# A decoder in one launch: ScalarE takes over the normalising of the state-space layer, and the passage to the next mixer is put in a new order

## The chip, the cores and the metric

One core of a Trainium2 chip runs the whole program. Its engines are named as in the profile: PE (TensorE, with its weight loads as PEld), DVE (VectorE), ACT (ScalarE), POOL (GpSimd) and SP (SyncE, which issues the DMAs). The metric is the device time of one execution in microseconds (us); lower is better.

## The reference

Six layers stand one behind the other, each as `x = layernorm(x + layer(x))`, on `x` of 16 batches, 128 tokens, 256 features. The fourth, the state-space layer, is the one that changes:

```python
zxbcdt = u @ W_in                                 # z, xBC, dt
xBC = silu(conv)                                  # causal conv of 4 taps
y, _ = ssd(x * dt[..., None], A * dt, Bh, Ch, 32)
y = y + x * D[None, None, :, None]
y = y.reshape(b, s, D_SSM) * silu(z)
var = jnp.mean(jnp.square(y), axis=-1, keepdims=True)
y = y * jax.lax.rsqrt(var + EPS) * norm_scale
return y @ W_out

def _layernorm(x, axis=-1, eps=1e-05):
    m = jnp.mean(x, axis=axis, keepdims=True)
    v = jnp.var(x, axis=axis, keepdims=True)
    return (x - m) / jnp.sqrt(v + eps)
```

The fifth layer, mixer two, multiplies keys and values per head, convolves them (a Toeplitz matrix product), multiplies by the query and sums. The sixth is a quantised feed-forward layer with a Hadamard transform.

## The kernel before

Everything is on chip: `X` holds the tokens of all 16 batches with tokens in the partitions, `XT` the same turned round. Each layer is a set of small functions, one per operation and engine, and each engine calls them in an order written out in the code. Engines work strictly in that order and meet only through semaphores: a function first waits for counts, then issues one instruction (or a few) that raises its own count. So an instruction that waits also holds up all that stands behind it on its engine.

The state-space layer works on groups of two batches. `step(i)` of an engine does the projection of group i (ten units on PE: six with the convolution's taps, four for the gate) and, beside it, the later parts of the groups before. Below, a is the first and b the second batch of the group whose scan step i prepares. The steps 2 to 7 run in a loop; `begin` and `end` write out what lies ahead of them and behind.

What happens to a batch in the parts that matter here, with lines of the profiled kernel:

- GpSimd makes the exponents (`args`, L1503) in a tile that lies in MIX. ScalarE clips them (`floor`, L1277) and takes the exponential (`decay`, L1283). VectorE multiplies by C times B (`matrix`, L1390). PE then scans (L1156).
- PE turns x back (L1135), ScalarE keeps it (`keep_xs`, L1271), GpSimd multiplies by dt (`x_dt`, L1537) and by D (`skip`, L1529).
- VectorE adds the skip (L1399) and multiplies by the gate (`gated`, L1408). ScalarE squares (L1290), GpSimd adds the squares in two instructions (`add_squares`, L1518 and L1520), PE sums (L1165), VectorE makes the variance (L1415) and GpSimd takes the root (`root`, L1511).
- PE multiplies by W_out (`out_product`, L1175), VectorE scales and adds X into tile Y (`residual`, L1423), then takes the statistics (L1429, L1435). GpSimd adds eps and takes the power -1/2 (`rstd`, L541 and L543). VectorE subtracts the mean and multiplies (`norm_x`, L549) from Y into X, with two Y tiles by turns. PE turns X (`x_turn`, L1185) and ScalarE keeps it in XT (L1296).
- In each unit ScalarE takes the product out of its bank with the fourth tap (`tap3`, L1249), and VectorE adds the three others (`taps`, L1376). The gate's units end in a Silu on ScalarE (L1258). Exp and Silu need different tables, so ScalarE loads a table twice per step.

In `end`, the last batches of the state-space layer are mixed with the first 18 of the 32 items of mixer two. An item is two products of keys and values on GpSimd (L632), six matmuls on PE (L655 to L657), two multiplications by the query (L673) and a sum (L684) on VectorE. Item 0 needs the first eight batches of XT, item 16 all of them. The keys' tile has three buffers. Behind item 17 the last layer begins, its first instruction on PE being L1616. That layer already normalises in the way that the change brings in (L1741 on ScalarE, L2040 on GpSimd).

The change touches tile Y and the new tile NR, `norm_x`, `residual`, `stats`, `aggregate`, `rstd`, and the three written orders of `step` and `end`.

Of the kernel before, what the change touches and what calls it, by code (L numbers as in the profile page):

```python
# [1054 lines left out]
def state_space(ch, T, d, s, before):  # L1055
# [38 lines left out]
    def tensor(pe):  # L1094
# [237 lines left out]

    def vector(dve):
# [83 lines left out]
        def residual(n):  # L1417
# [880 lines left out]
```

## Time and profile before

| | us |
|---|---|
| runs, median of 3 (lowest, highest) | 795.59 (793.16, 796.11) |
| profiled execution, device time | 795.49 |
| its span, first to last instruction | 793.5 |
| PE busy | 719.3 (91%) |
| DVE busy | 638.7 (80%) |
| POOL busy | 545.4 (69%) |
| ACT busy | 400.2 (50%) |
| state-space steps 2 to 7 | about 412 to 521 |
| passage to mixer two, to the first L1616 | 521 to 589.13 |

Busy shares are means over the whole program. In the two stretches named last several engines are nearly full at once, so what bounds them is read from the order of single instructions, not from the shares. Matmuls are pipelined and their ends are modelled, so PE's busy time is somewhat above its real need. A row of a timeline gives the start, the length, the instruction and, in brackets, the idle time ahead of it where that is long enough to be listed.

### The profile page before, as it was taken

To read this page: it belongs to the slowest core of one execution; us is meant where nothing else is said; L and a number is where in the kernel's file an instruction comes from. 1 tells how busy PE (TensorE), PEld (TensorE's weight loads), DVE (VectorE), ACT (ScalarE), POOL (GpSimd) and SP (SyncE) were. 2 spreads that over 40 slices of the span, in tenths; PEclk is the share of its full clock that TensorE was granted. 3 is DMA by queue.
4 is the path that set the end of the run, shared out by engine and by line. 5 is a ranking of instruction groups with operands and counts; after the bars stand their busy time and mean duration, and the time that the engine had idled before them with its cause. 6 is when DMAs were issued, how large, how long until landed. Compare 5 with 4: busy or idle time off the path is not lost. (4 is left out here: it accounts for less than half of the span.)

```text
span 793.5 us, 13405 instructions
## 1 busy us (share of the span) xinstructions
PE 719.3 (91%) x4263; PEld 496.9 (63%) x4286; DVE 638.7 (80%) x1291; ACT 400.2 (50%) x640; POOL 545.4 (69%) x785
## 2 busy tenths in 40 slices
PE   6999999999996999999859999989899898888894
PEld 5777777654442677776547777754444366666673
DVE  3878877789798777765859999969998989998754
ACT  0656566610614444444668778850100255777675
POOL 2768888977773443332147777799888788988882
PEclk9999999999998999999979999999999999999999
DMA  7900000000402300000121111103000000000001
GB/s 278 369 8 2 2 2 2 1 1 0 159 0 85 118 1 2 1 1 1 69 94 54 54 55 54 54 5 119 1 0 1 1 1 1 14 15 14 14 14 40
DMA packets 12868, 33.89 MB, mean 43 GB/s; under 512 B 2688, under 2 KB 8064, under 8 KB 11520
## 3 DMA queue, kind: packets, MB, share of 16 engines
q1 hardware_dynamic: 12800, 33.04, 11.5%
q8 instruction: 36, 0.59, 0.3%
q14 instruction: 32, 0.26, 0.1%
HBM read 30.88 MB, written 2.16 MB: 42 GB/s over the span
## 5 line engine op out<-in xcount | busy, mean ns | idle before, releaser
L1126 PE MATMUL bank<-XT,win_late 128*128 128x256 f32 x320 | 86.6, 397 | 5.7 <-DVE ss_xc L1376 5.4
L684 DVE TENSOR_REDUCE MIX<-m_pr 128x128 f32<-128x1024 f32 x64 | 77.4, 1211 | 0.7
L632 POOL TENSOR_TENSOR m_kv<-CTXT 128x512 f32<-128x512 f32 x64 | 65.0, 1039 | 10.4 <-PE bank L657 10.3
L632 POOL TENSOR_TENSOR m_kv<-XT,CTXT 128x512 f32<-128x512 f32 x64 | 67.7, 1082 | 4.2 <-PE bank L657 4.2
L1376 DVE SCALAR_TENSOR_TENSOR ss_xc<-bank,cw_late,ss_xc 128x254 f32<-128x254 f32 x144 | 66.5, 477 | 4.0 <-ACT ss_xc L1249 0.5
L1126 PEld LDWEIGHTS bank<-XT,win_late 128*128 128x128 f32 x320 | 56.1, 193 | 20.1 <-DVE ss_xc L1376 13.2
L655 PE MATMUL bank<-m_kv,toep 128*128 128x512 f32 x128 | 66.4, 600 | 1.9 <-POOL m_kv L632 1.3
L541 POOL TENSOR_TENSOR f_ve<-f_mv,eps 128x1 f32<-128x1 f32 x48 | 9.5, 198 | 81.7 <-DVE f_mv L946 61.1
L656 PE MATMUL bank<-m_kv,toep 128*128 128x512 f32 x128 | 65.4, 592 | 0.0
L657 PE MATMUL bank<-m_kv,toep 128*128 128x512 f32 x128 | 65.4, 592 | 0.0
L1686 PE MATMUL bank<-had_last,f_ht 128*128 128x256 f32 x256 | 60.7, 383 | 0.3 <-ACT f_ht L1763 0.2
L805 PE MATMUL bank<-wd,f_pmt 128*128 128x256 f32 x256 | 60.2, 382 | 0.0
L501 POOL TENSOR_TENSOR at_p<-at_p,at_mx 128x512 f32<-128x512 f32 x44 | 45.2, 1046 | 15.7 <-DVE at_mx L394 15.6
L1686 PEld LDWEIGHTS bank<-had_last,f_ht 128*128 128x128 f32 x256 | 47.4, 190 | 9.6 <-ACT f_ht L1763 2.2
L805 PEld LDWEIGHTS bank<-wd,f_pmt 128*128 128x128 f32 x256 | 46.7, 190 | 5.8
L1503 POOL TENSOR_TENSOR MIX<-CUM,MIX 128x1024 f32<-128x1024 f32 x16 | 30.3, 1900 | 26.1 <-DMA MIX<-cum_rows 18.9
L673 DVE TENSOR_TENSOR m_pr<-bank,XT 128x512 f32<-128x512 f32 x64 | 41.1, 685 | 8.4 <-PE bank L657 8.2
L673 DVE TENSOR_TENSOR m_pr<-bank,CTXT 128x512 f32<-128x512 f32 x64 | 40.8, 682 | 4.9 <-PE bank L657 4.4
L165 PE MATMUL bank<-XT,at_wqk 128*128 128x128 f32 x256 | 37.8, 299 | 6.7 <-DMA at_hmask<-hmask_dram 5.7
L657 PEld LDWEIGHTS bank<-m_kv,toep 128*128 128x128 f32 x128 | 24.3, 190 | 30.6 <-issue 30.6
L656 PEld LDWEIGHTS bank<-m_kv,toep 128*128 128x128 f32 x128 | 24.3, 190 | 30.6 <-issue 30.6
L317 ACT COPY at_pt<-bank 128x512 f32<-128x512 f32 x64 | 36.6, 590 | 11.3 <-PE bank L212 9.6
(237 smaller groups left out, 1899.6 us busy)
## 6 DMA issues: line engine op xcount, KB each, us to landing
MIX<-cum_rows SPq DMA_DIRECT2D x16, 512.0 KB, 3.7
toep<-toep_dram SPq DMA_DIRECT2D x2, 2048.0 KB, 11.8
X<-x_dram SPq DMA_DIRECT2D x1, 2048.0 KB, 12.7
CTXT<-ctxT_dram SPq DMA_DIRECT2D x1, 2048.0 KB, 17.6
out_dram<-f_o SPq DMA_DIRECT2D x16, 128.0 KB, 1.7
XT<-xT_dram SPq DMA_DIRECT2D x1, 1280.0 KB, 8.4
win_late<-win_dram SPq DMA_DIRECT2D x1, 1280.0 KB, 5.3
wgu<-wgu_dram SPq DMA_DIRECT2D x1, 1024.0 KB, 5.0
```

What stands on the lines that cost most here:

```text
L165: m = nc.tensor.matmul(b0[:, bass.ts(g, S)], wqk[:, c, bass.ts(g, P)], XT[:, c, tok(n)], start=(c == 0), stop=(c == C - 1))
L501: nc.gpsimd.tensor_tensor(v, v, MX[n % 2][:, 4 * t:4 * t + 4].unsqueeze(2).broadcast_to([P, 4, S]), ALU.subtract).then_inc(s["shifted"], 1)
L632: m = nc.gpsimd.tensor_tensor(KV[n % 3][:, c, :, :].rearrange("p (b j) i -> p b j i", b=HB), ki, vj, ALU.mult)
L655: nc.tensor.matmul(y[0][:, :], toep[:, a, 0:P], kv[0], start=True, stop=True)
L656: nc.tensor.matmul(y[1][:, :], toep[:, a, P:2 * P], kv[0], start=True, stop=False)
L657: nc.tensor.matmul(y[1][:, :], toep[:, a, 0:P], kv[1], start=False, stop=True).then_inc(s["conved"], 1)
L673: nc.vector.tensor_tensor(PR[n % 2][:, c, :, :].rearrange("p (b j) i -> p b j i", b=HB), bY[pair(n)][c][:, :].rearrange("p (b j i) -> p b ...
L684: nc.vector.tensor_reduce(head(MIX)[:, :, a, bass.ts(h, HB), :], PR[n % 2][:, :, :, :].rearrange("p c (b j) i -> p c b j i", b=HB), op=ALU ...
L805: m = nc.tensor.matmul(b6[:, 0:D], PMT[n % 2][:, r, :], wd[:, r, :], start=(r == 0), stop=(r == FC - 1))
L1126: m = nc.tensor.matmul(bX[(NU * g + n) % 3][:, 0:GS_], win[:, h, off:off + P], XT[:, h, bass.ts(g, GS_)], start=(h == 0), stop=(h == C - 1))
L1376: m = nc.vector.scalar_tensor_tensor(acc[:, :, sh:S], bank[:, :, 0:S - sh], cw[:, r, n:n + 1], acc[:, :, sh:S], ALU.mult, ALU.add)
L1686: m = nc.tensor.matmul(bV[k][:, bass.ts(r, 2 * P)], HT[:, 4 * k + 2 * r + i, :], had[:, i, :], start=(i == 0), stop=(i == 1))
```

## The change

1. `norm_x` leaves VectorE. GpSimd's `rstd` gets a third instruction, which makes -mean times the inverse deviation in a new tile NR (semaphore `offset`). ScalarE computes Y times scale plus offset into X with an Identity activation.
2. Y has three tiles instead of two, so `residual(n)` waits for the normalising of batch n-3 instead of n-2. The statistics wait until NR of two batches before is made.
3. In a step of ScalarE, `norm_x` of one batch stands between `tap3(i, 5)` and the second `keep_xs`, that of the other at the end of the step.
4. `end` has a new order on all four engines.

```diff
-    Y, ST, MV, VE, RS = two("y", [P, D]), two("st", [P, 6]), two("mv", [P, 2]), two("ve", [P, 1]), two("rs", [P, 1])
+    Y = [ch.sb(f"ss_y{k}", [P, D]) for k in range(3)]
+    NR, ST, MV, VE, RS = two("nr", [P, 1]), two("st", [P, 6]), two("mv", [P, 2]), two("ve", [P, 1]), two("rs", [P, 1])
 # scalar
+        def norm_x(n):
+            act.wait_ge(s["offset"], n + 1)
+            nc.scalar.activation(X[:, n, :], Y[n % 3][:, :], ACT.Identity, scale=RS[n % 2][:, :], bias=NR[n % 2][:, :]).then_inc(s["normed"], 1)
 # scalar, step
             tap3(i, 5)
+            norm_x(GB * (i - 3))
             keep_xs(GB * (i - 1) + 1)
...
             gate(i, 3)
+            norm_x(GB * (i - 3) + 1)
 # vector
-            upto(dve, s["normed"], n - 1)
-            nc.vector.scalar_tensor_tensor(Y[n % 2][:, :], bO[:, 0:D], RY[n % 2][:, :], X[:, n, :], ALU.mult, ALU.add).then_inc(s["out_free"], 1)
+            upto(dve, s["normed"], n - 2)
+            nc.vector.scalar_tensor_tensor(Y[n % 3][:, :], bO[:, 0:D], RY[n % 2][:, :], X[:, n, :], ALU.mult, ALU.add).then_inc(s["out_free"], 1)
 # vector, aggregate
+            upto(dve, s["offset"], n - 1)
 # vector, step
-            norm_x(GB * (i - 3))
-            norm_x(GB * (i - 3) + 1)
 # gpsimd, rstd
-            inv_std(pool, nc, T, MV[n % 2], VE[n % 2], RS[n % 2], T["eps5"], s["stats2"], s["eps_added"], s["rstd"], n)
+            upto(pool, s["normed"], n - 1)
+            k = n % 2
+            inv_std(pool, nc, T, MV[k], VE[k], RS[k], T["eps5"], s["stats2"], s["eps_added"], s["rstd"], n)
+            pool.wait_ge(s["rstd"], n + 1)
+            nc.gpsimd.tensor_scalar(NR[k][:, :], MV[k][:, 0:1], RS[k][:, :], -1.0, ALU.mult, ALU.mult).then_inc(s["offset"], 1)
 # tensor, end (first line of each)
-            scan(13); x_turn(6, 12); x_back(14); x_turn(7, 12); c_times_b(14); out_product(11); x_back(15); c_times_b(15); x_turn(8, 12); scan(14)
+            scan(13); x_turn(6, 12); x_back(14); c_times_b(14); x_turn(7, 12); out_product(11); x_turn(8, 12); c_times_b(15); x_back(15)
```

ScalarE, in the middle of a step. Names: L1249 (L1250 after) is `tap3`, L1277 (L1278) `floor`, L1271 (L1272) `keep_xs`, L1283 (L1284) `decay`. Before:

```order
L1271 COPY ss_xs<-bank 128x512
L1249 ACTIVATE ss_xc<-bank,cb_late,cw_late 128x256
L1277 ACTIVATE MIX<-MIX 128x1024
L1249 ACTIVATE ss_xc<-bank,cb_late,cw_late 128x256
L1271 COPY ss_xs<-bank 128x512
L1283 ACTIVATE MIX<-MIX 128x1024
```

After, where L1297 is the new normalising:

```order
L1250 ACTIVATE ss_xc<-bank,cb_late,cw_late 128x256
L1278 ACTIVATE MIX<-MIX 128x1024
L1250 ACTIVATE ss_xc<-bank,cb_late,cw_late 128x256
L1297 ACTIVATE X<-ss_y,ss_nr,ss_rs 128x256
L1272 COPY ss_xs<-bank 128x512
L1284 ACTIVATE MIX<-MIX 128x1024
```

The activation L1297 now stands ahead of the second `keep_xs` and so ahead of the `decay`, the table load and the square behind it.

PE, the beginning of the passage. L1156 (L1157 after) is `scan`, L1175 (L1176) `out_product`, L1185 (L1186) `x_turn`, L1135 (L1136) `x_back`, L1146 (L1147) `c_times_b`, L1165 (L1166) the sum of squares, L655 to L657 an item of mixer two. Before:

```order
L1135 MATMUL bank<-ident,ss_xc 128x128 x4
L1146 MATMUL bank<-ss_xc 128x128
L1185 MATMUL bank<-ident,X 128x128 x2
L1156 MATMUL bank<-MIX,wd 64x128 x8
L1175 MATMUL bank<-wout_late,ss_y 128x256 x4
L1156 MATMUL bank<-MIX,wd 64x128 x8
L1185 MATMUL bank<-ident,X 128x128 x2
L655 MATMUL bank<-m_kv,toep 128x512
L656 MATMUL bank<-m_kv,toep 128x512
L657 MATMUL bank<-m_kv,toep 128x512
```

After:

```order
L1136 MATMUL bank<-ident,ss_xc 128x128 x4
L1176 MATMUL bank<-wout_late,ss_y 128x256 x4
L655 MATMUL bank<-m_kv,toep 128x512
L656 MATMUL bank<-m_kv,toep 128x512
L657 MATMUL bank<-m_kv,toep 128x512
L1186 MATMUL bank<-ident,X 128x128 x2
L1157 MATMUL bank<-MIX,wd 64x128 x8
L1166 MATMUL bank<-ss_ones,ss_sq 128x1
L655 MATMUL bank<-m_kv,toep 128x512
L656 MATMUL bank<-m_kv,toep 128x512
L657 MATMUL bank<-m_kv,toep 128x512
L1157 MATMUL bank<-MIX,wd 64x128 x8
```

The item 0 of mixer two has moved ahead of both last scans, and item 1 stands between them.

GpSimd, the same place. L1503 (L1506 after) is `args`, L632 an item's product, L1537 (L1540) `x_dt`, L1529 (L1532) `skip`, L1511 (L1514) `root`, L1518 and L1520 (L1521 and L1523) `add_squares`. Before:

```order
L1503 TENSOR_TENSOR MIX<-CUM,MIX 128x1024 x2
L541 TENSOR_TENSOR ss_ve<-ss_mv,eps 128x1
L543 TENSOR_TENSOR ss_rs<-ss_ve,mhalf 128x1
L1537 TENSOR_TENSOR wd<-ss_xs,DT 128x512
L1511 TENSOR_TENSOR ss_ry<-ss_vy,mhalf 128x1
L1529 TENSOR_TENSOR wd<-ss_xc,dcol_late 128x512
L1537 TENSOR_TENSOR wd<-ss_xs,DT 128x512
L632 TENSOR_TENSOR m_kv<-XT,CTXT 128x512 x2
L1529 TENSOR_TENSOR wd<-ss_xc,dcol_late 128x512
L632 TENSOR_TENSOR m_kv<-XT,CTXT 128x512 x8
```

After:

```order
L1514 TENSOR_TENSOR ss_ry<-ss_vy,mhalf 128x1
L1506 TENSOR_TENSOR MIX<-CUM,MIX 128x1024
L632 TENSOR_TENSOR m_kv<-XT,CTXT 128x512 x2
L1506 TENSOR_TENSOR MIX<-CUM,MIX 128x1024
L1540 TENSOR_TENSOR wd<-ss_xs,DT 128x512
L1521 TENSOR_TENSOR ss_sq<-ss_sq 128x256
L1523 TENSOR_TENSOR ss_sq<-ss_sq 128x128
L632 TENSOR_TENSOR m_kv<-XT,CTXT 128x512 x2
L1532 TENSOR_TENSOR wd<-ss_xc,dcol_late 128x512
L1514 TENSOR_TENSOR ss_ry<-ss_vy,mhalf 128x1
L1540 TENSOR_TENSOR wd<-ss_xs,DT 128x512
L1532 TENSOR_TENSOR wd<-ss_xc,dcol_late 128x512
```

Item 0 now stands between the exponents of batch 14 and those of batch 15, and `rstd(10)`, L541 and L543, has gone behind item 5.

## Rows read from the trace of the kernel before

**Rows 1.** Windows: length, then busy us (instructions) of PE, PEld, DVE, ACT, POOL; clock.

```profile
484.63:502.94 18.31, 17.43 (x110) 14.03 (x109) 17.44 (x37) 14.66 (x23) 14.19 (x17) 1.00 0.16 58
...
521.24:589.13 67.89, 62.20 (x208) 33.32 (x207) 58.21 (x88) 10.94 (x19) 62.27 (x74) 0.97 0.12 36
```

**Rows 2.** Timeline, ScalarE, one group: start, length, instruction; in brackets idle time before, releaser.

```profile
484.66 1.06 ACT L1277 ACTIVATE MIX<-MIX 128x1024 f32<-128x1024 f32 x1 [2.02 <-POOL MIX L1503]
...
492.29 0.58 ACT L1249 ACTIVATE ss_xc<-bank,cb_late,cw_late 128x256 f32<-128x256 f32 x1
492.73 0.60 ACT L1271 COPY ss_xs<-bank 128x512 f32<-128x512 f32 x1
...
495.89 0.62 ACT L1290 ACTIVATE ss_sq<-ss_y 128x512 f32<-128x512 f32 x1
...
502.97 1.06 ACT L1277 ACTIVATE MIX<-MIX 128x1024 f32<-128x1024 f32 x1 [2.02 <-POOL MIX L1503]
```

**Rows 3.** Timeline, GpSimd, the same group.

```profile
491.17 1.04 POOL L1537 TENSOR_TENSOR wd<-ss_xs,DT 128x512 f32<-128x512 f32 x1 [1.91 <-ACT ss_xs L1271]
...
492.44 0.55 POOL L543 TENSOR_TENSOR ss_rs<-ss_ve,mhalf 128x1 f32<-128x1 f32 x1
...
494.67 0.54 POOL L1511 TENSOR_TENSOR ss_ry<-ss_vy,mhalf 128x1 f32<-128x1 f32 x1
496.59 0.75 POOL L1518 TENSOR_TENSOR ss_sq<-ss_sq 128x256 f32<-128x256 f32 x1 [1.38 <-ACT ss_sq L1290]
497.42 1.52 POOL L1520 TENSOR_TENSOR ss_sq<-ss_sq 128x128 f32<-128x128 f32 x1
...
500.17 0.91 POOL L543 TENSOR_TENSOR ss_rs<-ss_ve,mhalf 128x1 f32<-128x1 f32 x1
501.05 1.89 POOL L1503 TENSOR_TENSOR MIX<-CUM,MIX 128x1024 f32<-128x1024 f32 x1
```

**Rows 4.** Timeline, VectorE, the same group.

```profile
496.96 0.53 DVE L549 TENSOR_SCALAR X<-ss_y,ss_mv,ss_rs 128x256 f32<-128x256 f32 x1
497.41 1.21 DVE L1390 TENSOR_TENSOR MIX<-MIX,ss_cbm 128x1024 f32<-128x1024 f32 x1
...
499.99 0.68 DVE L1408 TENSOR_TENSOR ss_y<-ss_ysum,ss_sz 128x512 f32<-128x512 f32 x1
501.11 1.98 DVE L549 TENSOR_SCALAR X<-ss_y,ss_mv,ss_rs 128x256 f32<-128x256 f32 x1 [0.44 <-POOL ss_rs L543]
```

**Rows 5.** Instructions that touch f_nr: durations ns min/median/max, first and last start.

```profile
L2040 POOL TENSOR_SCALAR f_nr<-f_mv,f_rs x16: 264/264/809, 598.8 to 742.8; 128x1 f32<-128x1 f32 x16
L1741 ACT ACTIVATE X<-f_y,f_nr,f_rs x16: 589/601/612, 599.1 to 743.6; 128x256 f32<-128x256 f32 x16
```

**Rows 6.** Timeline, TensorE, the passage to mixer two and its end.

```profile
526.16 1.44 PE L1156 MATMUL bank<-MIX,wd 128*64 128x128 f32 x16 [2.92 <-DVE MIX L1390]
527.53 3.28 PE L1175 MATMUL bank<-wout_late,ss_y 128*128 128x256 f32 x8
...
559.40 0.41 PE L1185 MATMUL bank<-ident,X 128*128 128x128 f32 x2 [1.95 <-DVE ss_vy L1415]
...
565.05 0.41 PE L1185 MATMUL bank<-ident,X 128*128 128x128 f32 x2 [0.82 <-DVE ss_vy L1415]
...
586.56 1.02 PE L655 MATMUL bank<-m_kv,toep 128*128 128x512 f32 x2
...
589.13 0.38 PE L1616 MATMUL bank<-ident,MIX 128*128 128x128 f32 x2
```

**Rows 7.** Groups of instructions, GpSimd, 521 to 590 us: count, busy us, mean ns.

```profile
L632 POOL TENSOR_TENSOR m_kv<-XT,CTXT 128x512 f32<-128x512 f32 x41 | 43.5, 1084 | 3.2 <-PE bank L657 3.2
...
L543 POOL TENSOR_TENSOR ss_rs<-ss_ve,mhalf 128x1 f32<-128x1 f32 x6 | 3.3, 548 | 0.5
...
L1518 POOL TENSOR_TENSOR ss_sq<-ss_sq 128x256 f32<-128x256 f32 x4 | 2.9, 722 | 0.9 <-ACT ss_sq L1290 0.9
...
L1520 POOL TENSOR_TENSOR ss_sq<-ss_sq 128x128 f32<-128x128 f32 x4 | 1.8, 456 | 0.3
```

More of the change, by code:

```diff
@@ L1290, in square @@
             nc.scalar.activation(SQ[n % 2][:, :, :], Y2[n % 2][:, :, :], ACT.Square).then_inc(s["sq_made"], 1)
+        def norm_x(n):
+            if not 0 <= n < B:
+                return
+            act.wait_ge(s["offset"], n + 1)
+            nc.scalar.activation(X[:, n, :], Y[n % 3][:, :], ACT.Identity, scale=RS[n % 2][:, :], bias=NR[n % 2][:, :]).then_inc(s["normed"], 1)
         def keep_x(n):
@@ L1328, in end @@
         def end():
-            square(12); keep_x(6); keep_xs(14); keep_x(7); floor(14); decay(14); floor(15); decay(15); keep_xs(15); keep_x(8); square(13); keep_x(9)
-            keep_x(10); square(14); keep_x(11); square(15); keep_x(12); keep_x(13); keep_x(14); keep_x(15)
+            keep_x(6); keep_x(7); keep_xs(14); floor(14); square(12); decay(14); keep_x(8); floor(15); keep_xs(15); square(13); decay(15); keep_x(9)
+            square(14); norm_x(10); keep_x(10); norm_x(11); keep_x(11); norm_x(12); square(15); keep_x(12); norm_x(13); keep_x(13); norm_x(14)
+            keep_x(14); norm_x(15); keep_x(15)
         return step, begin, end
@@ L1433, in aggregate @@
                 return
+            upto(dve, s["offset"], n - 1)
             held(dve, s["stats1"], n + 1, T["dve_passed"])
             nc.vector.bn_aggr(MV[n % 2][:, :], ST[n % 2][:, :]).then_inc(s["stats2"], 1)
-        def norm_x(n):
-            if not 0 <= n < B:
-                return
-            norm(dve, nc, Y[n % 2], X[:, n, :], MV[n % 2], RS[n % 2], s["rstd"], s["normed"], n)
         def step(i):
@@ L1559, in end @@
         def end(mix):
-            args(14); args(15); rstd(10); x_dt(14); root(11); skip(14); x_dt(15); mix(0); skip(15); mix(1); mix(2); mix(3); mix(4); add_squares(12)
-            mix(5); rstd(11); add_squares(13); root(12); mix(6); rstd(12); mix(7); root(13); mix(8); add_squares(14); rstd(13); mix(9); root(14)
-            add_squares(15); mix(10); rstd(14); mix(11); root(15); mix(12); rstd(15); mix(13); mix(14); mix(15); mix(16); mix(17)
+            root(11); args(14); mix(0); args(15); x_dt(14); add_squares(12); mix(1); skip(14); root(12); x_dt(15); skip(15); mix(2); mix(3)
+            add_squares(13); mix(4); mix(5); rstd(10); root(13); add_squares(14); mix(6); rstd(11); mix(7); mix(8); root(14); rstd(12); rstd(13)
+            mix(9); add_squares(15); mix(10); mix(11); root(15); rstd(14); mix(12); rstd(15); mix(13); mix(14); mix(15); mix(16); mix(17)
         return step, end
@@ L2077 @@
       "sz_made y_made y1_made y2_made sq_made sq_half sq_added ss_made vy_made ry_made out_made out_free stats1 stats2 "
-      "eps_added rstd normed x_turned x_kept").split()
+      "eps_added rstd offset normed x_turned x_kept").split()
 F1 = ("consts mix_turned skip_made skip_free summed stats1 stats2 eps_added rstd offset normed peaks inv_made scaled shifted "
```

23 lines of the change are left out of this document (11 added, 12 removed).

## The prediction

> **What bounds the kernel now.** I read three things in this order. First the windows that cut the program where the change lies: one steady group takes 18.31 us, with PE busy 17.43, DVE 17.44, ACT 14.66 and POOL 14.19. The passage from 521.24 to 589.13 has PE at 62.20 and POOL at 62.27 of 67.89 [rows 1]. In the steady group two engines look full, so the shares don't say which one sets the pace, and I followed single instructions.
>
> The timeline of ScalarE from one `floor` to the next is the second view. `floor` starts at 484.66, right behind the end of `args` on POOL. The row for it lists 2.02 us of waiting for POOL [rows 2]. From there ScalarE runs to the end of the second square, 495.89 + 0.62 = 496.51, and its timeline shows no idle time in between: 11.85 us. POOL then waited 1.38 us for just that square, starts `add_squares` at 496.59 and works through `skip`, `rstd` and `args` until 501.05 + 1.89 = 502.94, without a listed gap [rows 3]. At 502.97 the next `floor` starts [rows 2]. 11.85 + 6.46 = 18.31 us, the whole period. So ScalarE and GpSimd together form a closed chain as long as the step, though each looks a quarter idle.
>
> The third view is VectorE. It waits 0.44 us for `rstd` and then spends 1.98 us in the second `norm_x` (501.11 to 503.09), which otherwise takes about 0.5. POOL's L1503 runs beside it from 501.05 to 502.94 [rows 3, 4], so most of the 1.98 is VectorE held up. The reverse is seen too: `add_squares`' second part takes 1.52 us beside `matrix` (497.41 + 1.21 = 498.62) [rows 3, 4], against 0.46 in the passage [rows 7]. The normalising costs VectorE 0.46 (496.96 to the next start, 497.41), 1.98 and the wait of 0.44, 2.9 us per step, and VectorE has just 0.9 us of free time. VectorE is thus a second bound, tied with the first.
>
> In the passage PE decides. It loses 2.92 us before `scan(14)` and runs the product behind it in 3.28 us instead of 1.9, at the lower of its two clock levels for a while. It loses 1.95 and 0.82 at two `x_turn` that wait for a variance [rows 6]. Together that is 2.92 + 1.4 + 1.95 + 0.82 = 7.1 us. The rest is convolutions at 2.57 us each (586.56 to 589.13 for the last).
>
> **The change part by part: the steps.** VectorE gets rid of 2.9 us per step and falls to about 15.4 of 18.31. PE needs at most its 17.43. If only these counted, steps would shorten. But the new work goes into the chain that has no slack.
>
> ScalarE's first `norm_x` stands behind the sixth `tap3`, and ahead of the second `keep_xs`. It waits for `offset`. `x_dt` runs from 491.17 to 492.21, and the power from 492.44 to 492.99 [rows 3]. The new instruction takes 0.26 [rows 5] and starts some 0.1 us later, so the offset is there at about 493.4. The `tap3` starts at 492.29, and `keep_xs` before started 0.44 later, at 492.73 [rows 2]. So ScalarE waits 0.7 us, and the activation of 0.60 [rows 5] adds 0.5 to the start of the next one, since neighbours overlap by 0.1. `keep_xs` starts at 493.9 instead of 492.73: **+1.2 us** in the chain. Behind it are queued `decay`, a table load, the gate, and the square for which POOL waits. Bounds: 0.5 if the offset were early, 1.3 if the power is held up as at 500.17 (0.91 instead of 0.55).
>
> GpSimd's `offset` of the second batch stands between `rstd` and `args`, in the chain: 0.26 and a semaphore of 0.1, **+0.36 us**. The one for the first batch lies in POOL's wait for ScalarE. ScalarE's other `norm_x` waits for that second offset, and ScalarE is then idle ahead of `floor` (2.02 us listed): 0.6 us under cover of `args`' 1.89, cost nothing. It delays the next first `tap3`, but VectorE has 2.9 us more time.
>
> What goes back: VectorE reaches `matrix` of the second batch 0.46 us earlier, while `add_squares` starts 1.2 later. The stall of 1.52 - 0.46 = 1.06 falls away, and I count a new one of 0.35 on its first part, whose start would meet the end of `matrix`. `rstd` keeps its 0.36 (0.91 against 0.55), since `gated` (499.99, 0.68) remains beside it [rows 3, 4]. That is **-0.7 us**. Bounds: -1.4 if both stalls vanish, 0 if both stay.
>
> Sum per step: 1.2 + 0.36 - 0.7 = +0.85 us, between 0.5 + 0.36 - 1.4 = -0.55 and 1.3 + 0.36 = +1.65. In the first of the four steps with a normalising the pipeline is still filling; I choose +0.3 for it, inside the bounds. Three full steps follow up to the last `args` of the loop: 3 x 0.85 + 0.3 = **+2.8 us** (-2 to +5.5).
>
> The Trainium skill ("ScalarE: Activation LUTs", Rules for kernel authors) advises VectorE for adds and multiplies and budgets about 0.3 us per activation plus 0.83 ns per element. For 256 elements that is an estimate of 0.51 us, below the 0.60 in rows 5; by it each insertion would be 0.1 shorter, 0.4 in all. Its advice speaks against this change, and the trace bears it out only by VectorE's 0.5 us where it is undisturbed.
>
> **The passage.** I count from the end of the last `args` of the loop (502.94). Before, item 17 ends on PE at 589.13 [rows 6], 86.2 us later. After: the POOL chain up to the second `offset` is 18.31 - 1.89 + 0.85 = 17.2, then `root` 0.54 and `args(14)` 1.89, 19.7 us. From there to the squares of batch 15, POOL has in its new order items 0 to 9 (10 x 2.1 from the 1084 ns of one half, started back to back), `args(15)` 1.9, two `x_dt` and two `skip` 4.2, four `add_squares` of 1.2, three `root` 1.65, and four `rstd` with offset 1.16 each, 4.6 [rows 3, 5, 7]: 38.1 us. That is 57.8. PE then does the sum of squares, nine items and three `x_turn`, 0.1 + 23.1 + 0.7, and ends at 81.8. Item 0 and one `out_product` now lie over PE's wait for `scan(14)`. PE without any wait needs 86.2 - 7.1 = 79.1, so POOL is the bound here and not PE. GpSimd gets six offsets of 0.36, 2.2 us, in this stretch, and items ahead of `args(15)`. VectorE loses six `norm_x` and has room. ScalarE was busy 10.94 of 67.89 [rows 1], so its six normalisings there lie beside idle time.
>
> 86.2 - 81.8 = 4.4; I take **-4.0 us**, as POOL's single instructions can be held up by `gated` and `matrix`. Bounds: 0 if a late offset or root costs again what is saved, -7.1 if all of PE's losses go. What follows just moves with item 17.
>
> **Sum.** The profiled execution took 795.49, 0.1 below the median of the runs, so its sum holds for the median. 795.5 + 2.8 - 4.0 = **794.3 us**. A difference of less than 0.5% (4 us) can't be told from none, so I forecast no measurable change.
>
> **Rivals.**
> - *VectorE was the real bound.* Then ScalarE's chain gives way and a step falls to PE's 17.4, or by as much as another us, since PE's ends are modelled: -0.9 to -1.9 in four steps, -5.5, and -4.0 in the passage: 786. For it speaks that VectorE is nearly full and waits little; against it the gapless 18.31 through ScalarE and POOL.
> - *The stalls go with the instruction.* With the two-port `norm_x` gone both POOL stalls vanish, and the step is 18.31 - 0.55 = 17.75: -2.2 over the steps, with -4.4 in the passage 788.9. Speaks for it that `norm_x` is the instruction with 1.98; against it that `matrix`, not `norm_x`, lay beside the 1.52. The Trainium skill ("SBUF – State Buffer", two separate sides) says that a VectorE instruction with two SBUF inputs or in a two-port mode and a GpSimd instruction take one port pair by turns, whoever starts first keeping it. The rows fit that. By it, `matrix` and `gated`, with two SBUF inputs each, go on colliding.
> - *Slower.* POOL has no gap from `args(14)` to item 11. Each item that comes late leaves PE waiting, and as at 527.53, PE then falls to the lower clock level, 1.4 us a time [rows 6]. If the insertion costs its full 1.65 in each step (+5.5) and the passage saves nothing, the time is 801. It decides from a delay of 4 us of POOL in the passage. For it: POOL at 62.27 of 67.89. Against: item 0 now needs nothing that is late.
> - *The change does nothing*, because the parts cancel at other sizes: 795.5, inside the same bound.
>
> **How the numbers follow.** My forecast and the cancelling case 0.52 together, VectorE as the bound 0.13, stalls gone 0.18, slower 0.17. Faster by over 0.5% means below 791.6: 0.13 + 0.18 and a little of my own case's edge, 0.33. Slower means above 799.6: the last case without its mild part, 0.15. Same: 0.52. The range goes from 787, the middle of the two faster cases, to 800, most of the slower one. My own case alone spans 791 to 798.
>
> **What would show it.** Right if the distance between two `floor` that start behind `args` is about 19.1 us in steps 4 to 6, with ScalarE waiting for POOL's `offset` at the first `norm_x` (0.7), VectorE with 2 to 3 us of idle time per step, and `add_squares`' second part near 0.46. Item 17 should end about 82 us after the last `args` of the loop, with PE waiting for POOL's items instead of `matrix` and the variances. Wrong if the steps get shorter than 18.0 (then the chain isn't what I take it for), or if PE shows new waits of over 3 us in the passage.

## The result, and the profile after

The changed kernel took 798.7 us (median of 11 runs, 796.17 to 799.42), the kernel before 794.89 beside it (11 runs, 793.03 to 797.56). The ratio is 1.0039, with an interval of 1.0022 to 1.0057: slower by 0.4%, where 794.3 us and no change were forecast. The profiled execution took 799.26, its span 797.5, 4.0 more than the span before.

To see where the 4.0 us arose, I cut both spans at three instructions that both kernels have: the first `args` of the loop shown here (POOL), the last pair of `args` in the loop, and the first `mix_turn` of the last layer (PE). The last two of them stand at 501.05 and 589.13 us before ([rows 3, 6]), and at 504.44 and 590.86 after. Windows of the kernel before, then of the changed kernel, the passage and the last layer (columns as in [rows 1]):

```profile
501.05:589.13 88.08, 81.01 (x330) 48.66 (x327) 77.47 (x124) 26.79 (x45) 78.34 (x91) 0.98 0.13 40
589.13:793.50 204.37, 174.25 (x936) 118.73 (x947) 167.27 (x350) 111.16 (x177) 162.27 (x247) 0.99 0.03 11
```
```profile
504.44:590.86 86.42, 80.51 (x324) 47.72 (x324) 70.41 (x114) 31.96 (x55) 80.47 (x99) 0.98 0.13 41
590.86:797.50 206.64, 178.21 (x949) 120.40 (x947) 166.68 (x350) 111.10 (x177) 161.67 (x247) 0.97 0.03 11
```

| us | before | after | difference | predicted |
|---|---|---|---|---|
| up to the first `args` at 426.58 / 426.99 | 426.58 | 426.99 | +0.4 | 0 |
| four steps, to 501.05 / 504.44 | 74.47 | 77.45 | +3.0 | +2.8 |
| passage, to 589.13 / 590.86 | 88.08 | 86.42 | -1.7 | -4.0 |
| last layer, the same code in both | 204.37 | 206.64 | +2.3 | 0 |

The first row is no effect of the change: over the 13 profiles without e4 this mark lay anywhere from 423.42 to 426.99, behind code that none of them alters.

**The steps.** ScalarE in one group of the changed kernel (timeline):

```profile
486.63 1.06 ACT L1278 ACTIVATE MIX<-MIX 128x1024 f32<-128x1024 f32 x1 [0.80 <-POOL MIX L1506]
...
494.25 0.58 ACT L1250 ACTIVATE ss_xc<-bank,cb_late,cw_late 128x256 f32<-128x256 f32 x1
495.85 0.60 ACT L1297 ACTIVATE X<-ss_y,ss_nr,ss_rs 128x256 f32<-128x256 f32 x1 [1.03 <-POOL ss_nr L1550]
496.36 0.56 ACT L1272 COPY ss_xs<-bank 128x512 f32<-128x512 f32 x1
...
499.48 0.63 ACT L1291 ACTIVATE ss_sq<-ss_y 128x512 f32<-128x512 f32 x1
...
506.36 1.06 ACT L1278 ACTIVATE MIX<-MIX 128x1024 f32<-128x1024 f32 x1 [0.80 <-POOL MIX L1506]
```

POOL in the same group, then VectorE's `gated` (L1418 after):

```profile
494.40 0.55 POOL L543 TENSOR_TENSOR ss_rs<-ss_ve,mhalf 128x1 f32<-128x1 f32 x1
495.05 0.77 POOL L1550 TENSOR_SCALAR ss_nr<-ss_mv,ss_rs 128x1 f32<-128x1 f32 x1
...
500.18 1.17 POOL L1521 TENSOR_TENSOR ss_sq<-ss_sq 128x256 f32<-128x256 f32 x1 [0.55 <-ACT ss_sq L1291]
501.43 0.46 POOL L1523 TENSOR_TENSOR ss_sq<-ss_sq 128x128 f32<-128x128 f32 x1
```
```profile
495.09 0.68 DVE L1418 TENSOR_TENSOR ss_y<-ss_ysum,ss_sz 128x512 f32<-128x512 f32 x1
```

`floor` to `floor` is 19.73 us. From the `tap3` to `keep_xs` it is 496.36 - 494.25 = 2.11, against 0.44 in [rows 2]: +1.67, the 1.03 of waiting for the offset and the activation. From the end of the square (500.11) to `args` (504.44) it is 4.33, against 4.54 in [rows 2, 3]. 1.67 - 0.21 = 1.46, and the step grew by 19.73 - 18.31 = 1.42. The window of this group shows VectorE busy 15.97 of 19.74 us, for 17.44 of 18.31 in [rows 1]: it has its free time, and the step has nothing from it.

```profile
486.57:506.31 19.74, 17.35 (x110) 14.15 (x109) 15.97 (x35) 15.63 (x25) 15.45 (x20) 1.00 0.16 54
```

**The passage.** POOL's groups of the changed kernel between the two marks; those of the kernel before beneath:

```profile
L632 POOL TENSOR_TENSOR m_kv<-XT,CTXT 128x512 f32<-128x512 f32 x40 | 41.4, 1064 | 0.0
...
L1521 POOL TENSOR_TENSOR ss_sq<-ss_sq 128x256 f32<-128x256 f32 x6 | 5.8, 964 | 0.5 <-ACT ss_sq L1291 0.5
L1532 POOL TENSOR_TENSOR wd<-ss_xc,dcol_late 128x512 f32<-128x512 f32 x4 | 5.1, 1284 | 0.0
...
L1550 POOL TENSOR_SCALAR ss_nr<-ss_mv,ss_rs 128x1 f32<-128x1 f32 x9 | 2.9, 320 | 0.9
```
```profile
L632 POOL TENSOR_TENSOR m_kv<-XT,CTXT 128x512 f32<-128x512 f32 x40 | 42.4, 1084 | 3.2 <-PE bank L657 3.2
...
L1518 POOL TENSOR_TENSOR ss_sq<-ss_sq 128x256 f32<-128x256 f32 x6 | 4.4, 726 | 2.3 <-ACT ss_sq L1290 2.3
L1529 POOL TENSOR_TENSOR wd<-ss_xc,dcol_late 128x512 f32<-128x512 f32 x4 | 4.1, 1035 | 0.0
```

The waits of POOL for PE (3.2 us) are gone: from 520 us to the last item POOL waits once, for 0.29 us. It is the bound, as forecast. But it is busy 2.1 us longer: nine offsets of 2.9, and 1.4 and 1.0 more in `add_squares` and `skip`, some of it given back elsewhere. It is the bound by little: PE's last wait, for POOL's squares of batch 15 at 566.58, is 0.37 us long, and PE had itself lost time to the lower clock level at 537 to 541 us. PE never waits for an item's products; its longest wait behind 520 us is 1.90.

The -1.7 of the passage is a difference of two profiles. The other profile of the kernel before that is unaltered up to here, e6 below, has 88.79 for 88.08; the other one of the changed kernel, e5, has 86.44 for 86.42. So the gain is 1.7 to 2.4 us.

**The last layer.** The same wait of PE for f_hmix, in the kernel before and in the changed one (timeline):

```profile
705.93 0.65 PE L1674 MATMUL bank<-ident,f_hmix 128*128 128x128 f32 x4 [1.97 <-POOL f_hmix L1985]
...
706.85 0.60 PE L1674 MATMUL bank<-ident,f_hmix 128*128 128x128 f32 x4
```
```profile
707.64 0.76 PE L1681 MATMUL bank<-ident,f_hmix 128*128 128x128 f32 x4 [1.95 <-POOL f_hmix L1992]
...
709.05 1.06 PE L1681 MATMUL bank<-ident,f_hmix 128*128 128x128 f32 x4
```

PE over 706 to 714 and 786 to 790 us, before and after (busy, granted clock, DMA share, GB/s):

```profile
706.00:714.00 8.00, 7.95 (x56) 1.00 0.03 9
786.00:790.00 4.00, 0.69 (x7) 0.95 0.20 68
```
```profile
706.00:714.00 8.00, 6.36 (x27) 0.79 0.06 19
786.00:790.00 4.00, 2.45 (x16) 0.57 0.10 35
```

The wait is as long, but TensorE's granted clock then falls from 2.4 to 1.2 GHz (it reads 0.50 over 709 to 711 us). Four transposes take 1.06 us instead of 0.60. It falls once more near the end, behind a wait that the kernel before has too (1.78 us at 782.43 there). PE's last matmuls before, then the wait and the last matmuls after:

```profile
785.64 1.05 PE L1707 MATMUL bank<-wd,f_wt 128*128 128x256 bf16 x8 [1.10 <-ACT f_wt L1785]
```
```profile
785.14 1.03 PE L1714 MATMUL bank<-wd,f_wt 128*128 128x256 bf16 x8 [1.78 <-DVE f_ydown L1935]
...
788.77 1.89 PE L1714 MATMUL bank<-wd,f_wt 128*128 128x256 bf16 x8 [1.10 <-ACT f_wt L1792]
```

### The profile page after: what moved, and what is told of

Read it like the earlier page. It is cut to its first block and busy times, and to the rows that moved or that the text cites. A ratio compares the mean times of both kernels' runs of the same rounds, so it can differ in the third digit from the quotient of the medians.

```text
span 797.5 us, 13458 instructions
## 1 busy us (share of the span) xinstructions
PE 723.9 (91%) x4286; PEld 498.5 (63%) x4286; DVE 625.2 (78%) x1275; ACT 408.0 (51%) x656; POOL 549.3 (69%) x801
## 5 line engine op out<-in xcount | busy, mean ns | idle before, releaser
L632 POOL TENSOR_TENSOR m_kv<-CTXT 128x512 f32<-128x512 f32 x64 | 65.0, 1039 | 10.4 <-PE bank L657 10.3
L655 PE MATMUL bank<-m_kv,toep 128*128 128x512 f32 x128 | 66.5, 601 | 2.0 <-POOL m_kv L632 1.3
L632 POOL TENSOR_TENSOR m_kv<-XT,CTXT 128x512 f32<-128x512 f32 x64 | 66.7, 1070 | 0.8 <-PE bank L657 0.8
L541 POOL TENSOR_TENSOR f_ve<-f_mv,eps 128x1 f32<-128x1 f32 x48 | 9.5, 198 | 83.5 <-DVE f_mv L946 61.1
L657 PE MATMUL bank<-m_kv,toep 128*128 128x512 f32 x128 | 66.3, 600 | 0.0
L1506 POOL TENSOR_TENSOR MIX<-CUM,MIX 128x1024 f32<-128x1024 f32 x16 | 30.3, 1895 | 26.2 <-DMA MIX<-cum_rows 18.9
L657 PEld LDWEIGHTS bank<-m_kv,toep 128*128 128x128 f32 x128 | 24.6, 192 | 31.0 <-issue 31.0
L656 PEld LDWEIGHTS bank<-m_kv,toep 128*128 128x128 f32 x128 | 24.3, 190 | 30.6 <-issue 30.6
```

Of the source, the lines that this page charges most:

```text
L632: m = nc.gpsimd.tensor_tensor(KV[n % 3][:, c, :, :].rearrange("p (b j) i -> p b j i", b=HB), ki, vj, ALU.mult)
L655: nc.tensor.matmul(y[0][:, :], toep[:, a, 0:P], kv[0], start=True, stop=True)
L656: nc.tensor.matmul(y[1][:, :], toep[:, a, P:2 * P], kv[0], start=True, stop=False)
L657: nc.tensor.matmul(y[1][:, :], toep[:, a, 0:P], kv[1], start=False, stop=True).then_inc(s["conved"], 1)
```

## The experiments

All parts of a span below lie between the same marks. Each row is one profiled execution, so only the parts are compared in it, and the times are medians of the timed runs against the kernel before on the same chip.

| kernel | steps | passage | last layer | falls of the clock in the last layer | time, us | ratio (95%) |
|---|---|---|---|---|---|---|
| before | 74.47 | 88.08 | 204.37 | none | | |
| after | 77.45 | 86.42 | 206.64 | f_hmix, tail | 798.70 | 1.0039 (1.0022 to 1.0057) |
| e1 | 77.53 | 89.28 | 205.47 | f_hmix | 799.83 | 1.0051 (1.0031 to 1.0071) |
| e2 | 74.50 | 89.34 | 206.70 | f_hmix, tail | 797.74 | 1.0039 (1.0015 to 1.0062) |
| e3 | 74.38 | 85.79 | 206.75 | f_hmix, tail | 794.94 | 0.9987 (0.9966 to 1.0007) |
| e4 | (75.99) | (90.80) | 205.25 | tail | 797.13 | 1.0024 (1.0006 to 1.0041) |
| e5 | 77.46 | 86.44 | 204.11 | none | 795.25 | 1.0010 (0.9993 to 1.0026) |
| e6 | 74.48 | 88.79 | 204.41 | none | 794.91 | 0.9995 (0.9979 to 1.0011) |
| e7 (e3 again) | 74.34 | 85.73 | 206.18 | f_hmix, tail | 794.78, one run | |
| e8 | 72.64 | 87.64 | 206.42 | f_hmix, tail | 793.29 | 0.9985 (0.9969 to 1.0001) |
| e9 | 72.63 | 84.78 | 203.94 | none | 788.63 | 0.9921 (0.9900 to 0.9942) |
| e10 | 73.74 | 85.72 | 204.06 | none | 791.91 | 0.9962 (0.9946 to 0.9978) |
| e11 | 74.47 | 91.46 | 204.10 | none | 797.53 | 1.0032 (1.0011 to 1.0052) |
| e12 | 77.45 | 85.14 | 203.92 | none | 792.96, one run | |

In e4 the marks of POOL stand elsewhere in the step. e11's passage holds its added transposes. "f_hmix" is the fall behind the first wait shown above, "tail" the one near the end. Each profile also shows the lower level behind PE's last instruction, where it costs nothing; the column leaves that out. In the passage the clock falls once in the profiles of the kernel before, the changed one, e2, e4, e5, e8 and e9, twice in e6 and e11, and not at all in e1, e3, e7, e10 and e12.

A timed run has only its mean clock over the whole program. That says how much clock a run lost, but not where: e7 has both falls in the last layer and reads 0.979, e11 has none there and reads 0.978. Runs are counted below as under or over 0.9785 with this limit.

**e1, the steps alone**: the new steps, with the orders of the passage from the kernel before (the normalising of the passage on ScalarE).

```
@@ TensorE
         def end(mix):
-            scan(13); x_turn(6, 12); x_back(14); c_times_b(14); x_turn(7, 12); out_product(11); x_turn(8, 12); c_times_b(15); x_back(15)
+            scan(13); x_turn(6, 12); x_back(14); x_turn(7, 12); c_times_b(14); out_product(11); x_back(15); c_times_b(15); x_turn(8, 12); scan(14)
...
```

> The changed steps with the old order of the passage (normalising on ScalarE throughout). Theory one, the closed chain over ScalarE and GpSimd: the step stays at 19.7 us against 18.3, so the steps cost +3 us, and the passage takes about the 88.1 us from the start of the loop's last args to the end of item 17 that it took before. Theory two, that the loss comes from the new passage: step 19.7 but total no slower than the changed kernel minus 2. The last layer takes 204.4 us if PE's clock holds at its 2 us wait, 206.6 if it falls there; theory three (clock) expects either of the two and nothing in between that isn't the clock.

**e2, the passage alone**: the steps of the kernel before, `norm_x` on VectorE throughout, the new orders of the passage.

```
@@ VectorE, against the changed kernel
-            residual(13); aggregate(12); add_up(3); add_up(4); times_q(5); variance(14); stats(13); aggregate(13); times_q(6); add_up(5); gated(15)
+            norm_x(10); residual(13); aggregate(12); add_up(3); add_up(4); times_q(5); variance(14); stats(13); aggregate(13); times_q(6); norm_x(11)
+            add_up(5); gated(15); add_up(6); residual(14); times_q(7); stats(14); aggregate(14); add_up(7); norm_x(12); times_q(8); norm_x(13)
...
```

> The old steps (normalising on VectorE) with the new order of the passage; Y has three tiles, and mean and inverse deviation four, so that VectorE's normalising can stand where the new order allows. Steps 18.3 us. Chain theory: the passage takes 86.4 us or less from the start of the loop's last args (GpSimd has no offsets there, 2.2 us less), so the kernel is 2 to 4 us faster than before unless the clock falls in the last layer (+2.3). Rival: the passage gains only with the normalising off VectorE, then it takes 88 or more.

The steps cost +3.06 us in e1 and nothing in e2, as in the sum. Both expectations missed the passage: e1 has 89.28 for the 88.1 expected, and in e2 the rival holds (88 or more), not the chain theory (86.4 or less). The last layer of e1 is a third value, 205.47: only the fall at f_hmix was there, and the expectation had not reckoned with two separate falls. The passage is a table of two by two: 88.08 with neither part, 89.28 with ScalarE's normalising and the old order, 89.34 with the new order and VectorE's, 86.42 with both. Neither part gains alone, and together they save 1.7. That the two mixed cells lie above 88.08 is not shown, since the unaltered passage also gave 88.79 (e6). In e2 PE waits for VectorE's `norm_x` at three `x_turn`:

```profile
552.71 0.44 PE L1187 MATMUL bank<-ident,X 128*128 128x128 f32 x2 [1.70 <-DVE X L549]
559.29 0.44 PE L1187 MATMUL bank<-ident,X 128*128 128x128 f32 x2 [0.99 <-DVE X L549]
...
571.22 0.44 PE L1187 MATMUL bank<-ident,X 128*128 128x128 f32 x2 [1.59 <-DVE X L549]
```

**e3, the normalising later**: the changed kernel, both `norm_x` of a step behind ScalarE's last gate.

```
             tap3(i, 5)
-            norm_x(GB * (i - 3))
             keep_xs(GB * (i - 1) + 1)
...
             gate(i, 3)
+            norm_x(GB * (i - 3))
             norm_x(GB * (i - 3) + 1)
```

> The changed kernel with ScalarE's first normalising of a step moved behind the last gate, next to the second one, where ScalarE waits for args anyway. Chain theory: the step falls by the 1.67 us that the insertion takes, from 19.74 to about 18.1, and the kernel gains some 5 us on the changed one. Rival (the stalls of the shared memory port set the step, not the insertion): the step stays above 19.

The steps fall by 3.07 us to 74.38, as short as those of the kernel before (74.47). The last one is 18.47 us, where about 18.1 was expected and the kernel before has 18.31; the time fell by 3.8 us, where some 5 were expected. ScalarE goes from the `tap3` straight to `keep_xs`, and the first `norm_x` lies in idle time:

```profile
492.34 0.58 ACT L1250 ACTIVATE ss_xc<-bank,cb_late,cw_late 128x256 f32<-128x256 f32 x1
492.79 0.61 ACT L1272 COPY ss_xs<-bank 128x512 f32<-128x512 f32 x1
...
499.44 0.59 ACT L1297 ACTIVATE X<-ss_y,ss_nr,ss_rs 128x256 f32<-128x256 f32 x1
```

The place of one instruction of 0.6 us is thus the whole cost of the steps. A second profile of this kernel, e7, repeats the steps, the passage, and both falls of the clock:

> A second look at the kernel with both normalisations behind the last gate, one profile: are its steps 18.1 to 18.3 us again, its passage 85.7, and does TensorE's clock fall in the last layer at the same two places? Theory A: yes for the steps and the passage, within 0.2 us; the two falls of the clock need not be the same.

**e4, `args` earlier on POOL** on top of e3.

```
-            args(GB * i)
+            if i == 0:
+                args(0)
...
             add_squares(GB * (i - 1) + 1)
+            args(GB * (i + 1))
             skip(GB * i + 1)
             rstd(GB * (i - 2) + 1)
```

> As the one before, and GpSimd issues the first args of the next group ahead of the second skip and rstd of this one, instead of behind them. Chain theory: skip 1.0, rstd 1.2 and offset 0.36 leave the chain, which falls to about 15.5, so PE's need (16.5 to 17.4) becomes the bound: step about 17, over 5 us gained on the one before. Rival (VectorE or PE is the bound already at 18): the step stays at 18.

A miss. A step is 499.05 - 479.54 = 19.51 us by POOL's `args`, where e3's is 501.26 - 482.79 = 18.47. As I read it (no run tests this apart), moving `args` forward puts 1.9 us ahead of `skip`, `rstd` and the offset, while ScalarE has the second `norm_x` in its queue ahead of the next group:

```profile
484.05 0.60 ACT L1297 ACTIVATE X<-ss_y,ss_nr,ss_rs 128x256 f32<-128x256 f32 x1 [3.25 <-POOL ss_nr L1550]
```

**e5 and e6, TensorE kept at work** in three waits of the last layer, in the changed kernel and in the one before.

```
         def h_turn(n, k):
+            if n == 7 and k == 1:
+                upto(pe, s["h1_kept"], n)
+                upto(pe, s["v1_kept"], n)
+                for r in range(16):
+                    nc.tensor.transpose(bH[k][:, bass.ts(r % 4, S)], ident[:, :], ident[:, :])
             pe.wait_ge(s["s2_made"], n + 1)
...
-            w_turn(14); down(13); down(14); w_turn(15); down(15)
+            w_turn(14); down(13); idle_work(14); down(14); w_turn(15); idle_work(8); down(15)
```

> The changed kernel, with TensorE kept at work in three waits of the last layer: 16 transposes of a constant ahead of the second h_turn of batch 7 (the wait of 1.95 us for f_hmix), 14 and 8 of them ahead of the last two rows of down. They write a bank that is free and that nobody reads then. Theory A (the last layer's +2.3 us are TensorE's clock, which falls after those waits): the clock reads 1.00 at about 706 to 714 us, and the layer from its first mix_turn to the end takes 205.4 us if only that one goes and 204.4 if both do, for 206.64; the time falls by 1 to 2.3 us, to 796.4 to 797.7. Rival B (the layer is longer for what it waits for, DVE, POOL or a DMA, and the low clock only goes along): the layer stays at 206.6 within 0.3, or grows by the transposes.

> The kernel before with the same three fillings. Theory A: in its profiled run the clock held at the f_hmix wait, so the layer keeps its 204.4 us; but of its timed runs a third read a mean clock of 0.976 at a median span of 794.9 and two thirds 0.98 and more at 792.85, so these runs are the ones that gain: the median falls by 0.3 to 1.0 us, and the spread between low-clock and other runs narrows. Rival B: no change or slower by the transposes.

The layer falls from 206.64 to 204.11, though PE now has 38 transposes more to do. Rival B is out. The timed runs agree: the ratio goes from 1.0039 to 1.0010, which is 2.3 us. PE at the wait, and its clock behind it, in e5:

```profile
703.54 1.91 PE L1676 MATMUL bank<-ident 128*128 128x128 f32 x16
705.70 0.66 PE L1686 MATMUL bank<-ident,f_hmix 128*128 128x128 f32 x4 [0.24 <-POOL f_hmix L2002]
...
706.62 0.60 PE L1686 MATMUL bank<-ident,f_hmix 128*128 128x128 f32 x4
```
```profile
706.00:714.00 8.00, 8.00 (x59) 1.00 0.01 3
```

In e6 the forecast fall of 0.3 to 1.0 us is not shown: the ratio is 0.9995, and its interval holds both no change and the forecast. Only the highest run went down, from 798.45 to 795.54. Its profiled layer had nothing to lose. With both kernels filled, the changed one is thus slower by 1.0010 against 0.9995, some 1.2 us, which fits +3.0 in the steps less 1.7 to 2.4 in the passage. The table gives the prices apart: no fall 203.9 to 204.4 us, f_hmix alone 205.5 (e1), the tail alone 205.3 (e4), both 206.2 to 206.8.

**e8, the offset on VectorE**, on top of e3: the three lines that make it leave POOL's `rstd` for a function of VectorE, called where its `norm_x` stood before.

```
-            pool.wait_ge(s["rstd"], n + 1)
-            nc.gpsimd.tensor_scalar(NR[k][:, :], MV[k][:, 0:1], RS[k][:, :], -1.0, ALU.mult, ALU.mult).then_inc(s["offset"], 1)
...
+        def offset(n):
+            dve.wait_ge(s["rstd"], n + 1)
+            nc.vector.tensor_scalar(NR[n % 2][:, :], MV[n % 2][:, 0:1], RS[n % 2][:, :], -1.0, ALU.mult, ALU.mult).then_inc(s["offset"], 1)
```

> The kernel with both normalisations behind the last gate, and the offset worked out on VectorE (one 128x1 operation) where the kernel before had its norm_x, no longer on POOL. Theory A (POOL bounds the passage: it has no idle time from 519 us to its end but 0.3): nine offsets leave it in the passage, 2.9 us of work and 0.9 of gaps before them, so the passage of 85.7 us falls by 2.5 to 3.8, less what VectorE or TensorE then bound; in the steps POOL's 2 x 0.4 us are beside other work or not, so 18.3 us or down to 17.9. Time: 794.9 less 2.5 to 4, so 791 to 792.5. Rival C (VectorE or TensorE is as near a bound as POOL): the passage falls by under 1 us and POOL waits for PE rows of mixer two as it did before (3 to 5 us of such waits). Rival D: VectorE waits for rstd and passes it on to gated: steps longer by 0.3 us or more.

Split: the steps gain 1.7 us more (0.43 a step), the passage loses 1.9. Theory A fails in the passage, and rival C had the reason but not the size: it expected a gain under 1 us with 3 to 5 us of POOL waiting for PE, and there are 1.5 us of such waits and 3.8 of waits for squares. The offset comes late from VectorE's full queue, PE waits for ScalarE's `norm_x`, and POOL waits for the square behind it.

```profile
556.98 0.73 POOL L1530 TENSOR_TENSOR ss_sq<-ss_sq 128x256 f32<-128x256 f32 x1 [2.45 <-ACT ss_sq L1291]
```
```profile
556.44 0.44 PE L1186 MATMUL bank<-ident,X 128*128 128x128 f32 x2 [1.50 <-ACT X L1297]
```

**e12, VectorE's matrix product cut short** for batches 14 and 15 (one head of eight).

```
-            nc.vector.tensor_tensor(LA[n % 2][:, :, :], LA[n % 2][:, :, :], CBM[n % 2][:, :].unsqueeze(1).broadcast_to([P, NH, S]),
+            heads = NH if n < 14 else 1
+            nc.vector.tensor_tensor(LA[n % 2][:, 0:heads, :], LA[n % 2][:, 0:heads, :], CBM[n % 2][:, :].unsqueeze(1).broadcast_to([P, heads, S]),
```

> The changed kernel, with VectorE's product of the decay matrix (matrix) of batches 14 and 15 cut to the first of its eight heads (the other seven are left unmultiplied): VectorE is busy 0.3 us there instead of 1.9. Theory A (POOL's operations of the passage are held up while VectorE does these): the POOL rows that took 1.71, 0.79 and 2.02 us beside it take 0.73, 0.46 and 1.04; the passage falls from 86.4 by the 2.3 us of them, less what another engine then bounds. Rival E (those POOL rows are long for another reason): they stay, and the passage falls by under 1 us.

POOL in the changed kernel, then in e12:

```profile
531.45 1.71 POOL L1521 TENSOR_TENSOR ss_sq<-ss_sq 128x256 f32<-128x256 f32 x1
533.23 0.79 POOL L1523 TENSOR_TENSOR ss_sq<-ss_sq 128x128 f32<-128x128 f32 x1
...
536.03 2.02 POOL L1532 TENSOR_TENSOR wd<-ss_xc,dcol_late 128x512 f32<-128x512 f32 x1
...
540.52 4.14 POOL L632 TENSOR_TENSOR m_kv<-XT,CTXT 128x512 f32<-128x512 f32 x4
```
```profile
529.15 0.78 POOL L1522 TENSOR_TENSOR ss_sq<-ss_sq 128x256 f32<-128x256 f32 x1
530.01 0.79 POOL L1524 TENSOR_TENSOR ss_sq<-ss_sq 128x128 f32<-128x128 f32 x1
...
532.81 1.08 POOL L1533 TENSOR_TENSOR wd<-ss_xc,dcol_late 128x512 f32<-128x512 f32 x1
...
536.37 4.14 POOL L632 TENSOR_TENSOR m_kv<-XT,CTXT 128x512 f32<-128x512 f32 x4
540.47 1.18 POOL L1522 TENSOR_TENSOR ss_sq<-ss_sq 128x256 f32<-128x256 f32 x1
```

VectorE's cut product still took longer than the 0.3 us expected, since it met a POOL instruction (`x_dt`, 528.15 to 529.19) in its turn:

```profile
528.30 1.04 DVE L1401 TENSOR_TENSOR MIX<-MIX,ss_cbm 128x128 f32<-128x128 f32 x1 [2.08 <-ACT MIX L1284]
```

1.71 becomes 0.78 and 2.02 becomes 1.08; the row of 0.79 stays, since it lay beside `gated` and not beside `matrix`. From the last loop `args` to the four items it is 34.23 us for 36.08: -1.85. Of that 0.46 goes back at once, because `add_squares` (1.18, after 0.72) now meets a `gated`, and the passage gains 1.3 in all. Rival E is out for these two rows. In e12 the clock did not fall in the passage either, and PE waits 1.19 us for the squares of batch 15, for 0.37 in the changed kernel. How much of the 1.3 would be left with the fall is not shown.

**e9 and e10, put together.** e10 is e3 with the fillings of e5. e9 moves besides the offset of batches 0 to 9 to VectorE and leaves that of 10 to 15 on POOL:

```
         def rstd(n):
+            if n == B - 6:
+                pool.wait_ge(s["normed"], n)
             inv_std(pool, nc, T, MV[k], VE[k], RS[k], T["eps5"], s["stats2"], s["eps_added"], s["rstd"], n)
+            if n >= B - 6:
                 pool.wait_ge(s["rstd"], n + 1)
```

> The kernel with both normalisations behind the last gate, with TensorE filled in the three waits of the last layer. Theory A: e3's layer of 206.75 us falls to 204.1 to 204.4, the time from 794.9 to 792.5 (ratio to the kernel before 0.996 to 0.997). Rival B (chance of the profiled runs): layer and time stay within 0.7 us of e3's.

> Put together from what the runs showed: both normalisations behind the last gate; the offset of batches 0 to 9 on VectorE (those of the steps), of batches 10 to 15 on POOL (those of the passage); the changed kernel's passage; TensorE filled in the three waits of the last layer. Theory A, with the parts as measured apart: steps 72.6 us (e8), passage 85.8 (e3), last layer 204.1 to 204.4 (e5, e6), after a start of 423 to 427 that differs by run: span 786 to 789.5, time 788 to 791, 0.5 to 0.8 per cent below the kernel before. Rival C: the passage grows as in e8 (87.6), and the time is 790 to 793.

Both came out as expected, e9 at the good end: 788.63 us, 0.8% below the kernel before, with the steps of e8, a passage of 84.78 (1 us shorter than expected; the reason is open) and a layer of 203.94. It beats both kernels.

**e11, the last layer moved by 1.6 us**: 15 transposes ahead of the first `mix_turn`, in the kernel before.

> The kernel before with 15 transposes of a constant ahead of the first mix_turn of the last layer: TensorE, which is busy there, begins the layer 1.6 us later, and nothing else changes. It asks what decides whether the clock falls at the f_hmix wait. If the place in time decides (theory P), the share of timed runs with a mean clock under 0.9785, 11 of 35 in the kernel before, becomes another one (most or none), and the time grows by 1.6 plus or minus 1. If each execution decides by itself (theory Q), the share stays near a third and the time grows by 1.6 us.

Nine of ten timed runs had a mean clock under 0.9785, against four of 21 of the kernel before on the same chip, and the time grew by 2.8 us. So the shares differ. But theory P is not shown by it: the profiled execution reads 0.978 and kept its clock at the f_hmix wait (1.99 us long there). It lost it elsewhere, in the passage, ahead of the shift. Where the other runs lost theirs is not on record. Behind the wait of 1.95 us at 559.40 [rows 6] PE goes on in the kernel before as in the first row; e11, in which nothing differs up to this point, as in those beneath:

```profile
560.50 1.02 PE L656 MATMUL bank<-m_kv,toep 128*128 128x512 f32 x2
```
```profile
559.33 0.41 PE L1185 MATMUL bank<-ident,X 128*128 128x128 f32 x2 [1.97 <-DVE ss_vy L1415]
...
560.49 1.92 PE L656 MATMUL bank<-m_kv,toep 128*128 128x512 f32 x2
```

So the same wait in the same code costs 1.7 us in one execution and nothing in another. Why a given kernel meets more of these falls than another stays open.

## Why the prediction was wrong

- **What bounds a step: right.** ScalarE and POOL form the closed chain. Taking 2.9 us a step from VectorE brought nothing (74.38 in e3, with `norm_x` off VectorE and out of ScalarE's full part, for 74.47 before). Taking 1.67 out of ScalarE's part gave 3.07 us back (e3), and taking the offset out of POOL's part another 1.74 (e8). VectorE as the real bound is refuted.
- **The steps, +2.8: right in sum, by two errors that cancel.** The insertion cost 1.67 and not 1.2: the offset was not there at 493.4 + 0.1, because POOL's new instruction took 0.77 instead of the 0.26 of [rows 5]. It started at 495.05, and VectorE's `gated` with its two SBUF inputs at 495.09. So it was in three steps out of three in which this offset took 0.77; no run takes `gated` away, so this cause is argued. I had bounded that at 1.3. POOL's part gave 0.21 back, where the sum had 0.7 less 0.36, 0.34. The step grew by 1.35 and 1.43, not 0.85. But only two steps did; the first two grew by -0.06 and +0.26, where I had 0.3 and 0.85.
- **`add_squares`' second part near 0.46: right** (501.43). The first part took 1.17 beside `matrix`, a stall of 0.42 where I chose 0.35.
- **The passage, -4.0: the mechanism right, the term mis-sized by 2.3.** POOL is the bound, without gaps. The count of its work was made with undisturbed durations. In the trace three of its rows took 1.71, 0.79 and 2.02 instead of 0.73, 0.46 and 1.04, 2.3 us, beside VectorE's `matrix` and `gated`; e12 shows the cause for the two large ones. The count against the trace: 20.3 us for 19.7 up to the end of `args(14)` (the insertion again), 39.9 for 38.1 from there to the squares of batch 15 (these rows, less items of 2.05 instead of 2.1), 24.3 for 23.9 on PE to the end. That is 84.5 for 81.8. I had named this risk and kept 0.4 us for it, though the new order of both engines can be laid side by side. The Trainium skill ("SBUF — State Buffer", SBUF: two separate sides) says that a VectorE instruction with two SBUF inputs and a GpSimd instruction that reads SBUF exclude each other. The trace agrees: POOL's products for mixer two (L632) at 540.52 to 544.66 lie beside VectorE instructions that read a bank, and keep their 1.04 each.
- **The sign "PE waits for POOL's items" did not come.** PE waited for the squares, for ScalarE's X and XT and once, 0.4 us, for `matrix`, never for an item's products, and no new wait was over 3 us. VectorE's idle time was 3.8 us a step, where 2 to 3 were expected.
- **"What follows just moves with item 17": the step that failed.** It was put at nothing without a look at the last layer. It was worth +2.3 us. The last layer's code is unchanged, and its waits are as long, but TensorE lost its clock behind two of them. I had priced such a fall in the passage, from [rows 6], and not looked for waits of the same kind behind it. With the waits filled (e5) the layer is back at 204.1, and the changed kernel is at 1.0010 (0.9993 to 1.0026), within the forecast of no measurable change, though the sum had it at 794.3 for 795.5, 0.9985. Of the changed kernel's timed runs ten of 11 had a mean clock under 0.9785, of the kernel before 11 of 35, 7 of 25 and 4 of 21. That these runs too lost it in the last layer is concluded from e5, where filling waits of that layer alone brought all ten runs to 0.979 or more. Why the changed kernel loses it so much more often is open, and could not be read from one trace.
- **The rival "slower"** gave 801 by full insertions and a passage that saves nothing. The sign was its, the mechanism for the most part another: it had falls of the clock, but in the passage, and the passage did save.
- **The rival "stalls go with the instruction"** is refuted: a stall of 0.42 stands in `add_squares`' first part. Its 17.75 us a step also held an error: with the insertion of 1.2 that the sum uses, all stalls gone would give 18.31 + 1.2 + 0.36 - 1.4 = 18.47.

## What to carry to other kernels

Before an instruction is put into a queue, ask what stands behind it in a closed chain: 0.6 us of work cost 1.4 to 1.7 us a step in one place, and nothing a few instructions later. When work is moved to POOL, lay its new order beside VectorE's and add the stall for each pair of instructions that both read two SBUF operands. A wait of about 2 us on TensorE was a risk of 1 to 1.7 us here, even where the code behind the change is the same. Constant transposes into a free bank, issued ahead of the wait, kept the clock up at the filled waits in all four profiles that have them.

## What was not expected of the hardware

- TensorE's clock fell behind waits of 1.8 to 2.0 us in some executions and not in others, with the same code and the same wait (559.40 in the kernel before, 559.33 in e11). What decides it no run shows.
- Transposes of a constant kept it up in the last layer: in e5, e6, e9 and e10 no profile has a fall there ahead of PE's end, and all 34 timed runs had a mean clock of 0.979 or more, though in the passage it still fell in three of the four profiles.
- The start of the loop, 425 us into the program, moves by up to 3.6 us from one profiled execution to the next without any change ahead of it. Spans of two single profiles can't be subtracted to a microsecond; their parts can.
